# Two normalised matrix layers on eight cores: one PSUM bank set, evictions on the scalar engine, a two-pass output stage, and output writes issued by GpSimd

## The chip, the cores and the metric

The kernel runs on one Trainium2 chip, the same program on all 8 cores, each on its own 2048 of the 16384 rows. The metric is the device time in microseconds of the slowest core. Engine names: PE is TensorE, DVE is VectorE, ACT is ScalarE, POOL is GpSimd, SP is SyncE. A letter q behind a name is the engine's own DMA queue or sequencer.

## The reference, cut to what matters

```
def ln(x): m = mean(x); v = var(x); return (x - m) / sqrt(v + 1e-5)      # over the last axis, 4096
x  = data                                   # [2, 8192, 4096] f32
w1 = weight1 * elem_mask                    # [4096, 4096]; mask in blocks of 32 x 32, a block counts if its sum is > 0
x  = x + ln( ln(x) @ w1.T )
x  = x + ln( ln(x) @ sign(weight2).T + bias )
return x                                    # [2, 8192, 4096] f32
```

## The kernel before

**Tiling.** A core has 2048 rows of x, worked in NCH = 4 chunks of TC = 512 rows, each of NT = 4 tiles of 128 rows (`tt` in the code, tiles 0 to 3 here). Each chunk goes through two layers (`layer` 0 and 1). A layer's weights are 16 slabs (`sl`) of 2 MB in bf16: slab `sl` holds one half (`kh = sl % 2`) of the contraction of 512 output columns (`nsl = sl // 2`). The two slabs of one `nsl` are called a group here, so a layer has groups 0 to 7. For each slab PE runs 4 tiles x 16 matmuls of 128x128 by 128x512 (line 462). A group's product stands in PSUM after the slab with `kh == 1`, one bank of 512 f32 columns per tile.

**PSUM.** All eight banks are used: `pmm` (four banks), `ptA` and `ptB` (two each). Even groups go to pmm. In all layers but the first of chunk 0 (`split`), odd groups go to ptA and ptB (`acc_bank`). ptA and ptB also take the transposes of the normalised rows, 16 per half tile (line 204), so the first transposes of a chunk wait for the last group's eviction (`prev_ev[0]["pt"]`).

**Weights.** Chunk 0 loads f32 weights in pieces of 512 KB through two staging buffers WST. In layer 0 DVE multiplies them with the expanded mask (line 375), in layer 1 ACT takes their sign (line 389); both write a slab buffer WSL (two of them) and POOL stores it to DRAM as c1m or c2m (line 400). Chunks 1 to 3 load these cached slabs, one DMA of 2 MB on SP's queue (line 415) into the buffer that was freed at the end of the slab before last.

**Front of a chunk.** x is loaded in halves of a tile into two buffers XS by POOL (line 517); DVE makes its statistics (lines 548 to 562, `emit_p0_part1`), ACT normalises into HS (lines 582, 586), PE transposes, ACT copies the transposes to HT (line 214). From chunk 1 on tile 0 of this is prepared during the layer before, and PE alternates transposes and the first slab's matmuls tile by tile.

**Eviction.** After a group's second slab DVE copies each tile's bank to ARAW, a bf16 buffer of 4 x 4096 columns (line 483 in layer 0, line 485 with the bias in layer 1), and then makes four statistics over them (line 492). Each evicted tile raises `vEv`; PE waits for it before it uses that bank again. Each finished tile of a group raises `vMM`.

**Between the layers** (`emit_a2`): DVE rescales ARAW, adds x (loaded again by POOL into XS, line 630) into XP, ACT makes sums of squares and the second normalisation.

**Output stage** (`emit_finalize`). At the end of a chunk the result is XP + normalised ARAW. A chain of small operations on DVE (`chain3`), then per tile three passes over 4096 columns on DVE: ARAW in place times a scalar (line 737), OS from XP minus a scalar (line 739), OS plus ARAW (line 742); then ACT issues the write of OS, 2 MB (line 748). OS is one buffer, so each tile waits for the previous tile's write (`sO`). The third pass raises `vFi`.

**Order.** The output stage of chunk c is emitted in layer 0 of chunk c + 1, after slab 0. On DVE it therefore stands behind the statistics of the new chunk's tiles 1 to 3 and ahead of the first eviction (group 0). That eviction waits for `vFi` of all four tiles, since it overwrites ARAW. The last chunk's output stage stands at the very end, by itself.

The rule by which a bank is chosen and guarded is:

```
prev_use = nsl - (2 if split else 1)
if prev_use >= 0:
    wt(t, ev_at.get((prev_use, tt)))
elif nsl == 0 and prev_ev[0] is not None:
    wt(t, prev_ev[0]["pm"][tt])
```

Of the kernel before, what the change touches and what calls it, by code (L numbers as in the profile page):

```python
# [5 lines left out]
try:  # L6
# [11 lines left out]
AF = mybir.ActivationFunctionType  # L18

D = 4096  # L20
TPC = 2048
NCH = 4
TC = TPC // NCH
NT = TC // 128
# [10 lines left out]
        "vDs", "vPs", "vMk", "vTp", "vBi", "vFi", "vXf"]  # L35


def build():
# [16 lines left out]
    with es:  # L55
# [373 lines left out]
        def emit_slab_mm(c, layer, sl, ready, su, ev_at, ht_mark, site,  # L429
                         pre_tt=None, tr_base=0, bank_guard=None):  # L430
            nsl, kh = sl // 2, sl % 2
            mm_marks = {}
            split = not (c == 0 and layer == 0)
# [4 lines left out]
            def _(t):  # L438
# [5 lines left out]
                for tt in range(NT):  # L444
                    if interleave:
                        pre_tt(t, tt)
                        if tt == 0:
                            wt(t, ready)
                    if kh == 0:
                        wt(t, ht_mark(tt))  # L450
                        if split and nsl % 2 == 1 and tt == 0:
                            wt(t, ht_mark(NT - 1))
                        prev_use = nsl - (2 if split else 1)
                        if prev_use >= 0:
                            wt(t, ev_at.get((prev_use, tt)))
                        elif nsl == 0 and prev_ev[0] is not None:
                            wt(t, prev_ev[0]["pm"][tt])
                    for j in range(KTS):
                        st_ap = HT[:, (kh * KTS + j) * 512 + tt * 128:
                                   (kh * KTS + j) * 512 + tt * 128 + 128]  # L460
                        mv_ap = WSL[su % 2][:, j * 512:(j + 1) * 512]
                        ins = t.matmul(acc_bank(split, nsl, tt),  # L462
                                       st_ap, mv_ap,
                                       start=(kh == 0 and j == 0),
                                       stop=(kh == 1 and j == KTS - 1))
                    if kh == 1 and tt < NT - 1:
                        mm_marks[tt] = inc(ins, "vMM", 1)
# [6 lines left out]
            if kh == 1:  # L474
                @blk.vector
                def _(v):
                    wt(v, ("vFi", state["og"]))
                    ins = None
                    for tt in range(NT):
                        wt(v, mm_marks[tt])  # L480
                        dst = ARAW[:, tt * D + nsl * 512: tt * D + (nsl + 1) * 512]
                        if layer == 0:
                            ins = v.tensor_copy(dst, acc_bank(split, nsl, tt))
                        else:
                            ins = v.tensor_tensor(dst, acc_bank(split, nsl, tt),  # L485
                                                  BIASF[:, nsl * 512:(nsl + 1) * 512],
                                                  op=OP.add)
                        ev_at[(nsl, tt)] = inc(ins, "vEv", 1)
                    wt(v, ev_at[(nsl, NT - 1)])
                    for tt in range(NT):  # L490
                        sslot = site * 4 + tt
                        ins = v.bn_stats(BNST[:, sslot * 48 + nsl * 6:  # L492
                                             sslot * 48 + (nsl + 1) * 6],
                                         ARAW[:, tt * D + nsl * 512:
                                              tt * D + (nsl + 1) * 512])
                    if nsl == 7:
                        ev_at["stats_done"] = inc(ins, "vDs", 1)
# [98 lines left out]
        def emit_a2(c, t0, ev_at):  # L596
# [25 lines left out]
            for tt in range(NT):  # L622
# [83 lines left out]
        def emit_finalize(c, ev_at):  # L706
            t0 = c * TC
# [14 lines left out]
            chain3 = ("vSt", cnt["vSt"])  # L722

            fin = {}
            for tt in range(NT):
                my_og = state["og"]
                state["og"] += 1

                @blk.vector
                def _(v, tt=tt, my_og=my_og):  # L730
                    wt(v, chain3)
                    if my_og > 0:
                        v.wait_ge(sem["sO"], 16 * my_og)
                    r3 = RS[:, 12 + tt:12 + tt + 1]
                    mrs3 = AUX[:, 12 + tt:12 + tt + 1]
                    srcr = ARAW[:, tt * D:(tt + 1) * D]
                    ins = v.tensor_scalar(srcr, srcr, r3, None, OP.mult)
                    vds_edge(v, ins)
                    ins = v.tensor_scalar(OS[:, :], XP[:, tt * D:(tt + 1) * D],
                                          mrs3, None, OP.subtract)  # L740
                    vds_edge(v, ins)
                    ins = v.tensor_tensor(OS[:, :], OS[:, :], srcr, op=OP.add)  # L742
                    fin[tt] = inc(ins, "vFi", 1)

                @blk.scalar
                def _(s, tt=tt):
                    wt(s, fin[tt])
                    s.dma_start(out_d[t0 + tt * 128: t0 + (tt + 1) * 128, :],
                                OS[:, :]).then_inc(sem["sO"], 16)
                    cnt["sO"] += 16  # L750

        fin_pending = [None]

        for c in range(NCH):
# [11 lines left out]
            for layer in range(2):  # L766
# [7 lines left out]
                def pre_tt(t, tt, _nm=norm_marks, _sp=single_pt, _c=c,  # L774
# [17 lines left out]
                for sl in range(NSL):  # L792
                    if sl + 1 < NSL:
                        nxt = emit_w_load_prep(c, layer, sl + 1)
                    ready, su = pend
                    emit_slab_mm(c, layer, sl, ready, su, ev_at, ht_mark, site,
                                 pre_tt=pre_tt if sl == 0 else None)
                    if sl == 0:
                        if layer == 0 and fin_pending[0] is not None:
                            emit_finalize(*fin_pending[0])  # L800
                            fin_pending[0] = None
# [7 lines left out]
                if single_pt:  # L809
                    prev_ev[0] = {"pm": {tt: ev_at[(7, tt)] for tt in range(NT)},  # L810
                                  "pt": None}
                else:
                    prev_ev[0] = {"pm": {tt: ev_at[(6, tt)] for tt in range(NT)},
                                  "pt": ev_at[(7, NT - 1)]}
# [50 lines left out]
```

## Time and profile before

| what | us |
|---|---|
| median of the 2 runs | 3339.06 (3338.13 to 3340.0) |
| the profiled execution | 3343.32 |
| its span, slowest core | 3341.9 |
| spans of the other cores | 3298.2 to 3338.4 |
| busy: PE, DVE, ACT, POOL | 2018.1, 890.5, 519.5, 339.9 |

The span runs from the first to the last instruction of a core; the execution's time lies 1.4 us above it. The page gives each engine's busy time over the whole span, but this kernel has stages of very different kinds: chunk 0 (to about 1510 us), where weights are prepared and PE waits for them, then three chunks of which each has a front, a steady layer 0, a stage between the layers and a steady layer 1, and a tail of 68 us. So times are to be read per stage. The mean granted TensorE clock is 0.818 to 0.824 of full speed on all cores.

### The profile page before, as it was taken

The page shows a single profiled execution, that of the slowest core. Times are in us where ns is not written, and L with a number is a line of the kernel's source. Part 1 is how long each engine was busy: PE and PEld are TensorE (multiplying, and loading weights), DVE is VectorE, ACT ScalarE, POOL GpSimd, SP SyncE. Part 2 cuts the span into 40 slices and gives each one's busy share as a digit, 9 for nine tenths or more (in the row PEclk, how much of TensorE's full clock was granted, in tenths as well). Part 3 has the DMA queues.
Part 4 walks back from the last instruction along what each step waited for, and adds up shares of the span by engine and source line. Part 5 has one row for each costly group of instructions (what it writes and reads, how often), then busy time and mean ns, then how long its engine had stood idle before and what let it go on. Part 6 is the DMA issues. An engine that isn't in the chain of part 4 may idle for free.

```text
span 3341.9 us, 24099 instructions; the slowest of 8 cores (3298.2 to 3341.9 us)
## 1 busy us (share of the span) xinstructions
PE 2018.1 (60%) x9272; PEld 930.2 (28%) x9272; DVE 890.5 (27%) x1412; ACT 519.5 (16%) x340; POOL 339.9 (10%) x328
## 2 busy tenths in 40 slices
PE   1033123322633555556895699689669968966991
PEld 0011011110211222223342344334234433423440
DVE  0132122211441100105313221531322144132114
ACT  0120000000025333333002400300240030024000
POOL 4404432343000000000000000000000000000000
PEclk9996567755866777778998899799879989977996
DMA  3456566555743777775544244454424445442442
GB/s 126 129 192 203 192 233 203 165 197 194 237 149 119 222 232 244 220 239 164 203 152 149 105 154 180 166 202 151 151 101 151 176 167 211 151 151 76 151 151 101
DMA packets 72944, 573.12 MB, mean 171 GB/s; under 512 B 8800, under 2 KB 8816, under 8 KB 42112
## 3 DMA queue, kind: packets, MB, share of 16 engines
q1 hardware_dynamic: 51840, 343.96, 31.4%
q0 software_dynamic: 18688, 194.08, 16.7%
q10 hardware_dynamic: 2304, 33.56, 2.5%
q8 instruction: 75, 1.23, 0.2%
q14 instruction: 37, 0.30, 0.0%
HBM read 470.86 MB, written 100.70 MB: 171 GB/s over the span
## 4 chain that ended last, share of the span: by engine, by line
PE 37%; DMA 28%; DVE 12%; ACT 10%; POOL 8%; issue 5%; DVEq 0%; POOLq 0%; ACTq 0%; SPq 0%
PE pmm L462 17%; DMA WST<-w2s 11%; PE ptA L462 9%; PE ptB L462 9%; DMA WST<-w1s 8%; POOL MHI L250 7%; DMA OS<-mask 3%; DMA out<-OS 3%; DVE WSL L375 2%; DVE OS L742 2%; ACT WSL L389 2%; DMA XS<-x 2%; ACT HS L693 2%; ACT HS L662 2%; DVE BNST L548 1%
## 5 line engine op out<-in xcount | busy, mean ns | idle before, releaser
L462 PE MATMUL pmm<-WSL,HT 128*128 128x512 bf16 x4608 | 1103.1, 404 | 279.7 <-ACT WSL L389 105.6
L462 PEld LDWEIGHTS pmm<-WSL,HT 128*128 128x128 bf16 x4608 | 470.8, 103 | 900.0 <-issue 424.8
L462 PE MATMUL ptA<-WSL,HT 128*128 128x512 bf16 x1792 | 409.8, 388 | 105.7 <-ACT WSL L389 104.9
L462 PE MATMUL ptB<-WSL,HT 128*128 128x512 bf16 x1792 | 395.9, 379 | 0.0
L274 PE MATMUL ptB<-COLRED,P4T 128*4 128x512 bf16 x8 | 4.7, 585 | 498.9 <-ACT COLRED L264 498.9
L204 PE MATMUL ptA<-IDN,HS 128*128 128x128 bf16 x576 | 63.8, 299 | 347.8 <-ACT HS L693 237.3
L462 PEld LDWEIGHTS ptA<-WSL,HT 128*128 128x128 bf16 x1792 | 177.8, 100 | 330.0 <-issue 129.0
L462 PEld LDWEIGHTS ptB<-WSL,HT 128*128 128x128 bf16 x1792 | 175.1, 98 | 211.6
L375 DVE TENSOR_TENSOR WSL<-WST,BTE 128x1024 bf16<-128x1024 f32 x128 | 155.5, 1223 | 208.6 <-DMA WST<-w1s 207.6
L389 ACT ACTIVATE WSL<-WST 128x1024 bf16<-128x1024 f32 x128 | 135.0, 1056 | 264.6 <-DMA WST<-w2s 264.4
L485 DVE TENSOR_TENSOR ARAW<-pmm,BIASF 128x512 bf16<-128x512 f32 x64 | 44.0, 691 | 447.9 <-PE pmm L462 447.9
L492 DVE BATCH_NORM_STATS2 BNST<-ARAW 128x6 f32<-128x512 bf16 x256 | 158.3, 681 | 6.6
L204 PEld LDWEIGHTS ptA<-IDN,HS 128*128 128x128 bf16 x576 | 55.6, 138 | 361.8 <-issue 361.8
L662 ACT ACT_TABLE_LOAD x16 | 20.5, 1283 | 864.5 <-DVE XP L655 864.2
L274 PEld LDWEIGHTS ptB<-COLRED,P4T 128*4 128x4 bf16 x8 | 0.6, 80 | 503.3 <-issue 503.3
L250 POOL TENSOR_TENSOR MHI<-MHI 128x1024 int32<-128x1024 int32 (+3 forms) x128 | 125.9, 984 | 18.3
L264 ACT ACT_TABLE_LOAD x8 | 10.3, 1283 | 741.3 <-POOL MHI L250 741.3
L485 DVE TENSOR_TENSOR ARAW<-ptA,BIASF 128x512 bf16<-128x512 f32 x32 | 22.1, 692 | 373.8 <-PE ptA L462 373.8
L288 DVE TENSOR_SCALAR BRT<-ptB 4x512 bf16<-4x512 f32 x8 | 5.4, 679 | 434.6 <-PE ptB L274 434.6
L548 DVE BATCH_NORM_STATS2 BNST<-XS 128x6 f32<-128x512 f32 x128 | 78.4, 679 | 142.1 <-DMA XS<-x 142.1
L630 POOL DMA_DIRECT2D XS<-x x32 | 19.3, 602 | 947.9 <-DVE XP L655 883.2
L214 ACT ACTIVATE HT<-ptA 128x2048 bf16<-128x2048 bf16 x36 | 67.6, 1877 | 277.5 <-PE ptA L204 277.5
(64 smaller groups left out, 1034.9 us busy)
## 6 DMA issues: line engine op xcount, KB each, us to landing
WSL<-c1m SPq DMA_DIRECT2D x48, 2048.0 KB, 9.3
WSL<-c2m SPq DMA_DIRECT2D x48, 2048.0 KB, 7.8
WST<-w1s SPq DMA_DIRECT2D x128, 512.0 KB, 4.7
WST<-w2s SPq DMA_DIRECT2D x128, 512.0 KB, 4.6
XS<-x POOLq DMA_DIRECT2D x56, 1024.0 KB, 6.0
OS<-mask POOLq DMA_DIRECT2D x16, 2048.0 KB, 10.1
XP<-mask POOLq DMA_DIRECT2D x16, 2048.0 KB, 12.7
c1m<-WSL POOLq DMA_DIRECT2D x16, 2048.0 KB, 10.4
```

The costliest lines, as they stand in the source:

```text
L204: ins = t.transpose(pt[:, j * 128:(j + 1) * 128], HS[:, ktg * 128:(ktg + 1) * 128], IDN[:, :])
L214: ins = eng.activation(dst, src, AF.Identity)
L250: ins = g.tensor_tensor(MHI[:, dst_off:dst_off + dst_n], a[:, :, 0], a[:, :, 1], op=OP.add)
L375: ins = v.tensor_tensor(dst, src, mk, op=OP.mult)
L389: ins = s.activation(buf[:, j0 * 512:(j0 + KTQ) * 512], WST[(wfirst + q) % 2][:, :], AF.Sign)
L462: ins = t.matmul(acc_bank(split, nsl, tt), st_ap, mv_ap, start=(kh == 0 and j == 0), stop=(kh == 1 and j == KTS - 1))
L485: ins = v.tensor_tensor(dst, acc_bank(split, nsl, tt), BIASF[:, nsl * 512:(nsl + 1) * 512], op=OP.add)
L492: ins = v.bn_stats(BNST[:, sslot * 48 + nsl * 6: sslot * 48 + (nsl + 1) * 6], ARAW[:, tt * D + nsl * 512: tt * D + (nsl + 1) * 512])
L548: ins = v.bn_stats(bn[:, (hf * 4 + q) * 6: (hf * 4 + q + 1) * 6], xb[:, q * 512:(q + 1) * 512])
L662: ins = s.activation(HS[:, :], XP[:, tt * D:(tt + 1) * D], AF.Square, accum_out=XSQ[:, tt:tt + 1])
L693: ins = s.activation(HS[:, :], XP[:, tt * D:(tt + 1) * D], AF.Identity, bias=AUX[:, 8 + tt:8 + tt + 1], scale=RS[:, 8 + tt:8 + tt + 1])
L742: ins = v.tensor_tensor(OS[:, :], OS[:, :], srcr, op=OP.add)
```

## The change

- `acc_bank` always returns a bank of pmm; ptA and ptB hold transposes only. PE waits for the eviction of the group before (`prev_use = nsl - 1`), tile by tile, and the transposes' extra wait is gone.
- In layer 0 of chunks 1 to 3 ACT evicts (`activation`, Identity) and DVE makes only the statistics. In layer 1, and in chunk 0, DVE evicts as before.
- The eviction of a tile waits for `vFi` of the same tile of the output stage (`fin_war`), no longer for all four. `vFi` is now raised by the first pass; a new semaphore `vFo` is raised by the second, and the stage between the layers and the write wait for that.
- The output stage has two passes per tile: OS = ARAW times a scalar, and OS = (XP minus a scalar) plus OS in one `scalar_tensor_tensor`. ARAW is no longer written by it.
- The write of OS is issued by POOL, no longer by ACT.
- The output stage is emitted in two parts, the small chain before slab 0 and the four tiles before slab 1.

```diff
-        def acc_bank(split, nsl, tt):
-            if split and nsl % 2 == 1:
-                return (ptA if tt < 2 else ptB)[:, (tt % 2) * 512:
-                                                (tt % 2 + 1) * 512]
+        def acc_bank(use8, nsl, tt):
             return pmm[:, tt * 512:(tt + 1) * 512]
...
-                        if split and nsl % 2 == 1 and tt == 0:
-                            wt(t, ht_mark(NT - 1))
-                        prev_use = nsl - (2 if split else 1)
+                        prev_use = nsl - 1
                         if prev_use >= 0:
                             wt(t, ev_at.get((prev_use, tt)))
                         elif nsl == 0 and prev_ev[0] is not None:
-                            wt(t, prev_ev[0]["pm"][tt])
+                            wt(t, prev_ev[0][tt])
...
             if kh == 1:
-                @blk.vector
-                def _(v):
-                    wt(v, ("vFi", state["og"]))
-                    ins = None
-                    for tt in range(NT):
-                        wt(v, mm_marks[tt])
...
+                og4 = state.get("og_pend", -NT)
+
+                def fin_war(eng, tt):
+                    if og4 + tt + 1 > 0:
+                        eng.wait_ge(sem["vFi"], og4 + tt + 1)
+
+                if layer == 0 and c >= 1:
+                    @blk.scalar
+                    def _(s):
+                        for tt in range(NT):
+                            fin_war(s, tt)
+                            wt(s, mm_marks[tt])
+                            dst = ARAW[:, tt * D + nsl * 512:
+                                       tt * D + (nsl + 1) * 512]
+                            ins = s.activation(dst, acc_bank(use8, nsl, tt),
+                                               AF.Identity)
+                            ev_at[(nsl, tt)] = inc(ins, "vEv", 1)
+
+                    @blk.vector
+                    def _(v):
+                        wt(v, ev_at[(nsl, NT - 1)])
+                        ins = None
+                        for tt in range(NT):
+                            sslot = site * 4 + tt
+                            ins = v.bn_stats(BNST[:, sslot * 48 + nsl * 6:
...
+                        vds_edge(v, ins)
...
+                else:
+                    @blk.vector
+                    def _(v):
+                        ins = None
+                        for tt in range(NT):
+                            fin_war(v, tt)
+                            wt(v, mm_marks[tt])
...
-                    wt(v, ("vFi", state["og"]))
+                    wt(v, ("vFo", state["og"]))
...
+        def emit_finalize_tile(c, chain3, tt):
...
+            @blk.vector
+            def _(v, tt=tt, my_og=my_og):
+                wt(v, chain3)
+                if my_og > 0:
+                    v.wait_ge(sem["sO"], 16 * my_og)
...
+                ins = v.tensor_scalar(OS[:, :], srcr, r3, None, OP.mult)
+                araw_free = inc(ins, "vFi", 1)
+                wt(v, araw_free)
+                ins = v.scalar_tensor_tensor(OS[:, :], XP[:, tt * D:(tt + 1) * D],
+                                             mrs3, OS[:, :],
+                                             OP.subtract, OP.add)
+                fin[tt] = inc(ins, "vFo", 1)
+
+            @blk.gpsimd
+            def _(g, tt=tt):
+                wt(g, fin[tt])
+                g.dma_start(out_d[t0 + tt * 128: t0 + (tt + 1) * 128, :],
+                            OS[:, :]).then_inc(sem["sO"], 16)
...
-                    ins = v.tensor_scalar(srcr, srcr, r3, None, OP.mult)
-                    vds_edge(v, ins)
-                    ins = v.tensor_scalar(OS[:, :], XP[:, tt * D:(tt + 1) * D],
-                                          mrs3, None, OP.subtract)
-                    vds_edge(v, ins)
-                    ins = v.tensor_tensor(OS[:, :], OS[:, :], srcr, op=OP.add)
-                    fin[tt] = inc(ins, "vFi", 1)
-
-                @blk.scalar
-                def _(s, tt=tt):
-                    wt(s, fin[tt])
-                    s.dma_start(out_d[t0 + tt * 128: t0 + (tt + 1) * 128, :],
-                                OS[:, :]).then_inc(sem["sO"], 16)
...
-                    if tt == 0 and prev_ev[0] is not None:
-                        pt_m = prev_ev[0].get("pt")
-                        if pt_m is not None:
-                            extra.append(pt_m)
...
+                    if layer == 0 and fin_pending[0] is not None:
+                        fc, fev = fin_pending[0]
+                        if sl == 0:
+                            fin_chain[0] = emit_finalize_chain(fc, fev)
+                        elif sl == 1:
+                            for ftt in range(NT):
+                                emit_finalize_tile(fc, fin_chain[0], ftt)
+                            fin_pending[0] = None
```

How this moves instructions is seen at three places of the front of chunk 1. First PE, from the end of group 0 (slab 1) to slab 2, before:

```order
L462 MATMUL pmm<-WSL,HT 128x512 [waits sWs1]
L462 MATMUL pmm<-WSL,HT 128x512 x63
L437 UNCONDITIONAL_BRANCH
L462 MATMUL ptA<-WSL,HT 128x512 [waits sWs0,vTe]
L462 MATMUL ptA<-WSL,HT 128x512 x15
L462 MATMUL ptA<-WSL,HT 128x512 [waits vTe]
L462 MATMUL ptA<-WSL,HT 128x512 x15
```

The same place after:

```order
L456 MATMUL pmm<-WSL,HT 128x512 [waits sWs1]
L456 MATMUL pmm<-WSL,HT 128x512 x63
L433 UNCONDITIONAL_BRANCH
L456 MATMUL pmm<-WSL,HT 128x512 [waits sWs0,vTe,vEv]
L456 MATMUL pmm<-WSL,HT 128x512 x15
L456 MATMUL pmm<-WSL,HT 128x512 [waits vTe,vEv]
L456 MATMUL pmm<-WSL,HT 128x512 x15
```

Slab 2's matmuls go to pmm and wait for evictions (`vEv`) before each tile's 16; before they waited for none.

Second, DVE around the last tile of the output stage and the first eviction, before:

```order
L737 TENSOR_SCALAR ARAW<-ARAW,RS 128x4096 [waits vSt,sO]
L739 TENSOR_SCALAR OS<-XP,AUX 128x4096 [waits vDs]
L742 TENSOR_TENSOR OS<-OS,ARAW 128x4096 [waits vDs]
L475 UNCONDITIONAL_BRANCH
L483 CAST ARAW<-pmm 128x512 [waits vFi,vMM]
L483 CAST ARAW<-pmm 128x512 [waits vMM] x3
L492 BN_STATS BNST<-ARAW 128x6 [waits vEv]
```

DVE at the same place after:

```order
L765 TENSOR_SCALAR OS<-ARAW,RS 128x4096 [waits vSt,sO]
L768 SCALAR_TENSOR_TENSOR OS<-XP,AUX,OS 128x4096 [waits vFi]
L487 UNCONDITIONAL_BRANCH
L493 BN_STATS BNST<-ARAW 128x6 [waits vEv]
L493 BN_STATS BNST<-ARAW 128x6 x3
```

The evictions have left DVE's queue. On ACT they stand where the four writes stood, behind the last copies of transposes; ACT after:

```order
L609 ACTIVATE HS<-XS,AUX,RS 128x2048 [waits vSt,vTr]
L613 ACTIVATE HS<-XS,AUX,RS 128x2048
L214 ACTIVATE HT<-ptA 128x16x128 [waits vTr]
L214 ACTIVATE HT<-ptB 128x16x128 [waits vTr]
L476 UNCONDITIONAL_BRANCH
L483 ACTIVATE ARAW<-pmm 128x512 [waits vFi,vMM] x4
```

So ACT evicts each tile when both its matmuls and its first pass of the output stage are done.

Third, POOL after the loads of x for the new chunk's tiles 1 to 3 (x6); before, the loads of x for the stage between the layers follow at once:

```order
L517 DMA XS<-x 128x2048 [waits vXf] x6
L623 UNCONDITIONAL_BRANCH
L630 DMA XS<-x 128x2048 [waits vXf] x2
L623 UNCONDITIONAL_BRANCH
L630 DMA XS<-x 128x2048 [waits vXf] x2
```

And POOL after, the last two of the four writes of the output stage, which stand between them:

```order
L776 DMA out<-OS 128x4096 [waits vFo]
L773 UNCONDITIONAL_BRANCH
L776 DMA out<-OS 128x4096 [waits vFo]
L650 UNCONDITIONAL_BRANCH
L657 DMA XS<-x 128x2048 [waits vXf] x2
```

The loads for the stage between the layers now stand behind the four writes.

## Rows read from the trace of the kernel before

**Rows 1.** Head of the page.

```profile
span 3341.9 us, 24099 instructions; the slowest of 8 cores (3298.2 to 3341.9 us)
```

**Rows 2.** Busy time by stage: front, layer 0 of chunk 1, tail; columns in the first row.

```profile
core 3: us, PE busy (x) PEld busy (x) DVE busy (x) ACT busy (x) POOL busy (x), PEclk, DMA share, GB/s
...
1510.00:1625.00 115.00, 74.58 (x384) 37.62 (x384) 58.92 (x88) 26.82 (x14) 3.70 (x6) 0.83 0.59 201
1625.00:1794.00 169.00, 168.74 (x768) 75.76 (x768) 37.51 (x59) 0.00 (x0) 0.00 (x0) 0.98 0.40 150
...
3274.00:3342.00 68.00, 0.18 (x1) 0.00 (x0) 38.47 (x33) 0.00 (x0) 0.00 (x0) 0.52 0.29 123
```

**Rows 3.** Timeline of PE: start, us, instructions, [idle before, ended by].

```profile
1510.86 1.05 PE L204 MATMUL ptA<-IDN,HS 128*128 128x128 bf16 x16 [1.05 <-DVE ARAW L485]
...
1625.27 30.73 PE L462 MATMUL pmm<-WSL,HT 128*128 128x512 bf16 x128 [11.34 <-DVE ARAW L483]
...
1683.46 27.79 PE L462 MATMUL pmm<-WSL,HT 128*128 128x512 bf16 x128
```

**Rows 4.** Chain of waits, chunk 1's front: start, us, what.

```profile
1586.95 14.04 DMA out<-OS
...
1609.44 6.45 DMA out<-OS
```

**Rows 5.** Timeline of DVE, last tile of the output stage, first eviction.

```profile
1615.98 1.29 DVE L737 TENSOR_SCALAR ARAW<-ARAW,RS 128x4096 bf16<-128x4096 bf16 x1 [6.62 <-DMA out<-OS]
1617.38 2.35 DVE L739 TENSOR_SCALAR OS<-XP,AUX 128x4096 f32<-128x4096 bf16 x1
1619.83 4.42 DVE L742 TENSOR_TENSOR OS<-OS,ARAW 128x4096 f32<-128x4096 f32 x1
1624.43 2.48 DVE L483 CAST ARAW<-pmm 128x512 bf16<-128x512 f32 x4 [0.17 <-DVE OS L742]
```

**Rows 6.** Timeline of DVE, fronts of chunks 2 and 3, waits for a write.

```profile
2183.00 1.28 DVE L737 TENSOR_SCALAR ARAW<-ARAW,RS 128x4096 bf16<-128x4096 bf16 x1 [8.80 <-DMA out<-OS]
...
2203.69 1.29 DVE L737 TENSOR_SCALAR ARAW<-ARAW,RS 128x4096 bf16<-128x4096 bf16 x1 [12.41 <-DMA out<-OS]
...
2791.61 1.29 DVE L737 TENSOR_SCALAR ARAW<-ARAW,RS 128x4096 bf16<-128x4096 bf16 x1 [13.32 <-DMA out<-OS]
```

**Rows 7.** Busy time and granted clock just after PE's idle stretch, columns as rows 2.

```profile
1625.20:1628.70 3.50, 3.44 (x9) 1.24 (x10) 3.40 (x6) 0.00 (x0) 0.00 (x0) 0.50 1.01 426
```

**Rows 8.** Timeline of DVE in the tail, first passes of tiles 0 and 1.

```profile
3282.51 1.28 DVE L737 TENSOR_SCALAR ARAW<-ARAW,RS 128x4096 bf16<-128x4096 bf16 x1 [0.18 <-DVE AUX L182]
...
3297.29 1.28 DVE L737 TENSOR_SCALAR ARAW<-ARAW,RS 128x4096 bf16<-128x4096 bf16 x1 [6.50 <-DMA out<-OS]
```

**Rows 9.** Chain of waits: a load issued by POOL, a write by ACT.

```profile
1525.04 0.50 issue
...
3290.84 0.03 issue
3290.87 6.33 DMA out<-OS
```

**Rows 10.** DMAs issued by POOL: XP from mask, then times to landing for mask, XS.

```profile
XP<-mask POOLq DMA_DIRECT2D x16, 2048.0 KB, 12.7
...
DMA to landing us min/median/max: 8.1/10.1/21.9
...
DMA to landing us min/median/max: 4.9/6.1/21.2
```

**Rows 11.** The page's groups: an ACT pass over 1024 elements.

```profile
L389 ACT ACTIVATE WSL<-WST 128x1024 bf16<-128x1024 f32 x128 | 135.0, 1056 | 264.6 <-DMA WST<-w2s 264.4
```

**Rows 12.** DMA issues at 1565 to 1575 us: slab 2's load.

```profile
WSL<-c1m SPq DMA_DIRECT2D x1, 2048.0 KB, 14.2
```

**Rows 13.** Timelines: PE in layer 1 of chunk 0, DVE's statistics of a tile.

```profile
1314.11 15.49 PE L462 MATMUL pmm<-WSL,HT 128*128 128x512 bf16 x64 [12.60 <-ACT WSL L389]
...
1513.11 4.83 DVE L548 BATCH_NORM_STATS2 BNST<-XS 128x6 f32<-128x512 f32 x8
```

More of the change, by code:

```diff
@@ L421, in emit_w_load_prep @@
             return ready, su
-        def acc_bank(split, nsl, tt):
-            if split and nsl % 2 == 1:
-                return (ptA if tt < 2 else ptB)[:, (tt % 2) * 512:
-                                                (tt % 2 + 1) * 512]
+        def acc_bank(use8, nsl, tt):
             return pmm[:, tt * 512:(tt + 1) * 512]
         def emit_slab_mm(c, layer, sl, ready, su, ev_at, ht_mark, site,
-                         pre_tt=None, tr_base=0, bank_guard=None):
+                         pre_tt=None, use8=False, tr_base=0, bank_guard=None):
             nsl, kh = sl // 2, sl % 2
             mm_marks = {}
-            split = not (c == 0 and layer == 0)
             interleave = pre_tt is not None and c >= 1
@@ L474, in emit_slab_mm @@
             if kh == 1:
-                @blk.vector
-                def _(v):
-                    wt(v, ("vFi", state["og"]))
-                    ins = None
-                    for tt in range(NT):
-                        wt(v, mm_marks[tt])
[L481 to L497, printed above, removed]
@@ new lines, in emit_slab_mm @@
+                og4 = state.get("og_pend", -NT)
[20 more added lines that the diff above has]
+                            ins = v.bn_stats(BNST[:, sslot * 48 + nsl * 6:
+                                                 sslot * 48 + (nsl + 1) * 6],
+                                             ARAW[:, tt * D + nsl * 512:
+                                                  tt * D + (nsl + 1) * 512])
+                        vds_edge(v, ins)
+                        if nsl == 7:
+                            ev_at["stats_done"] = ("vDs", cnt["vDs"])
+                else:
[5 more added lines that the diff above has]
+                            wt(v, mm_marks[tt])
+                            dst = ARAW[:, tt * D + nsl * 512:
+                                       tt * D + (nsl + 1) * 512]
+                            if layer == 0:
+                                ins = v.tensor_copy(dst, acc_bank(use8, nsl, tt))
+                            else:
+                                ins = v.tensor_tensor(dst, acc_bank(use8, nsl, tt),
+                                                      BIASF[:, nsl * 512:(nsl + 1) * 512],
+                                                      op=OP.add)
+                            ev_at[(nsl, tt)] = inc(ins, "vEv", 1)
+                        wt(v, ev_at[(nsl, NT - 1)])
+                        for tt in range(NT):
+                            sslot = site * 4 + tt
+                            ins = v.bn_stats(BNST[:, sslot * 48 + nsl * 6:
+                                                 sslot * 48 + (nsl + 1) * 6],
+                                             ARAW[:, tt * D + nsl * 512:
+                                                  tt * D + (nsl + 1) * 512])
+                        if nsl == 7:
+                            ev_at["stats_done"] = inc(ins, "vDs", 1)
@@ L704, in emit_a2, with emit_finalize_chain @@
             return a2_norm
[L706 to L707 removed]
+        def emit_finalize_chain(c, ev_at):
+            state["og_pend"] = state["og"]
             @blk.vector
@@ L797, in build @@
                                  pre_tt=pre_tt if sl == 0 else None)
[L798 to L801, printed above, removed]
                     if c == 0 and layer == 0 and sl % 2 == 0 and sl // 2 + 2 <= 7:
@@ L807, in build @@
                         pend = nxt
[L809 to L814, printed above, removed]
+                prev_ev[0] = {tt: ev_at[(7, tt)] for tt in range(NT)}
                 if layer == 0:
```

28 lines of the change are left out of this document (14 added, 14 removed).

## The prediction

> **What bounds the kernel now.** I read four views, in this order: the head of the page, the busy time by stage, the chain of waits around one suspicious stage, and then the timeline of PE (TensorE) and of DVE (VectorE) in that stage. The span is 3341.9 us on the slowest core [rows 1]. The profiled execution took 3343.3 us with what lies around the span, and the median of the runs shown is 3339.06 us, 4.3 us less.
>
> The stages say where the change can matter [rows 2]. In the long stretches in which the sixteen slabs of a layer run from the cached weights, PE is busy all the time (168.74 of 169 us). There DVE works 37.5 us and ACT (ScalarE) not at all, so whoever evicts there is hidden. In the front of chunk 1 (1510 to 1625 us) PE is busy only 74.58 of 115 us, and in the tail (3274 to 3342 us) it does nothing. The fronts of chunks 2 and 3 look alike. So the change must be judged at three fronts and one tail.
>
> In a front PE first works through group 0 (slabs 0 and 1, in bank set pmm), then group 1 (slabs 2 and 3, in ptA and ptB), and then it stops. Group 2 starts at 1625.27, after 11.34 us of idleness ended by DVE's first eviction [rows 3]. That eviction stands on DVE behind the whole output stage of the previous chunk: four tiles, each of three passes, with only one buffer OS. So each tile waits for the previous tile's write: the chain goes through writes of 14.04 and 6.45 us [rows 4]. DVE's last tile begins at 1615.98, its passes last 1.29, 2.35 and 4.42 us, and the eviction begins at 1624.43 [rows 5]. What bounds a front is this ladder of passes and writes, and the two bank sets let PE do two groups, 128 matmuls beyond group 0, beside it.
>
> **Part 1: one bank set instead of two.** Group 1 now goes to pmm too, so slab 2 needs, tile by tile, the evictions of group 0. In the steady stretches this costs nothing. Tile 0 of a group is finished three tiles before its slab ends; three tiles are 48 matmuls, some 10.4 us at 27.79 us for 128 [rows 3], and one eviction lasts 0.62 us (2.48 for four, [rows 5]). The cover is these 10.4 us; it is gone only if the evicting engine is late by more. In layer 1 DVE takes in tile 0 of the next chunk between two groups, eight statistics (4.83 us, [rows 13]) and a short chain, and that falls into a slab which gives it no eviction. In chunk 0, layer 1, PE waits for weights before each slab anyway, as 12.60 us before slab 9 [rows 13]. I take nothing for both.
>
> In the fronts it costs. Tile 3 of slab 2 cannot start before tile 3 of ARAW has been read by the last tile of the output stage. Behind that moment PE still has tile 3 of slab 2 and all of slab 3, 16 + 64 = 80 matmuls, before it comes to group 2. These had been done beside the ladder. At 27.79/128 = 0.217 us each they are 17.3 us: **+17.3 us per front**. The price of the cold clock stays: after the idle stretch the granted clock is 0.50 of full speed, that is the 1.2 GHz level [rows 7], and the first group takes 30.73 instead of 27.79. This 2.9 us is paid once either way, since a second, earlier stall lies before the wait for the last tile and its slow matmuls are hidden in it.
>
> **Part 2: the eviction's guard and its engine.** The eviction waited for all three passes of all four tiles; now each tile waits for the first pass of its own. From the start of the last tile that is 2.35 + 0.10 = 2.45 us instead of 1624.43 − 1615.98 = 8.45: **−6.0 us per front**. That ACT now evicts is neutral: its 1024-element pass takes 1.056 us [rows 11], so half of it lies between 0.53 and 1.06, against DVE's 0.62 to 0.69. I take 0.65. ACT has nothing queued behind these evictions until the end of the layer. The guard is per tile only because ACT is not behind DVE's passes in order; DVE's statistics still are, and nobody waits for them there.
>
> **Part 3: two passes instead of three.** The removed in-place pass costs 1.40 us a tile with its gap (1617.38 − 1615.98). The new first pass, bf16 to f32 with one scalar, is the form of the old second one, 2.35 us. The new second pass (subtract and add in one, bf16 and f32 in, f32 out) stands in no row. From below it is a pass of 2.35, from above the two old passes together, 6.8; nearest is the old addition with the same two inputs, 4.42 [rows 5], and I take that. Three tiles are on the path of a front, four on the tail's: **−4.2 us per front, −5.6 in the tail**.
>
> The Trainium skill's "Vector Engine (DVE) Microarchitecture Reference" (section "Points that are easy to get wrong") says that this instruction halves its throughput when both SBUF sources are not bf16. Here XP is bf16, so by the rule nothing is halved, which no row of this trace can confirm.
>
> **Part 4: the write is issued by POOL (GpSimd) instead of ACT.** Two things change per write. An ACT write starts 0.03 us after its release; a load on POOL starts 0.50 us after [rows 9]. And the landing: ACT's write of 2 MB lands in 6.33 us when nothing else runs [rows 9]. POOL's loads of 2 MB took at least 8.1 us and those of 1 MB at least 4.9 [rows 10]. So the landing grows by something between 0 and 1.8 us; half of 6.33 for the second megabyte on top of 4.9 gives 8.0 as a ceiling, and I take 7.4, +1.1. Together +1.6 us per write, with ends 0 and 2.3. On the path are three writes in each front, four in the tail: **+4.8 us per front, +6.4 in the tail**.
>
> The Trainium skill ("DMA: Bandwidth & Descriptors", section "Anatomy of one DMA — SWDGE (gpsimd) path") fits such a transfer as 2.0 us plus bytes over 436 GB/s. By estimate that is 6.8 us for 2 MB, so the write would grow by 1.0 us and not 1.6, and the whole sum would be 8 us less. The row of 4.9 us for 1 MB stands 0.5 above the same fit (4.4), so the trace leans to the dearer value.
>
> POOL's queue also holds the x loads for the second half of the layer (two of 1 MB); they stood ahead and now stand behind the four writes. They are needed some 170 us later. Nothing is lost there.
>
> **Part 5: who shares the DMA engines.** In chunks 2 and 3 DVE waited 12.41 and 13.32 us for the third write [rows 6], because slab 4's weights (issued at the end of slab 2) came at the same time; in chunk 1 it waited 6.62 us [rows 5]. Now PE is held inside slab 2, so slab 4's load is issued only after the ladder. The third write runs alone: **−5.8 us in chunk 2, −6.7 in chunk 3**. In its place slab 4's load meets the fourth write and the x loads. A contended weight load took 14.2 us [rows 12]; between the end of slab 2 and that of slab 3 lie 13.8 us and a little cold clock, so this costs 0 to 3 us per front; I take 0.
>
> **Part 6: the transposes' guard.** They waited 1.05 us for DVE's last eviction [rows 3], three times. The front's ladder starts on DVE's own statistics, behind that same eviction, which do not move. Zero.
>
> **The sum.** Chunk 1: 17.3 − 6.0 − 4.2 + 4.8 = +11.9. Chunk 2: 11.9 − 5.8 = +6.1. Chunk 3: 11.9 − 6.7 = +5.2. Tail: the tile's period was 14.78 us (3297.29 − 3282.51, [rows 8]), now −1.4 + 1.6 each, four times: +0.8. In all **+24.0 us**: 3343.3 becomes 3367.3 by the profiled execution, and 3339.06 becomes **3363** by the median. That is 0.7% slower.
>
> **The rivals.**
> A, not slower: the new second pass runs at 2.35 us, not 4.42. Its place is each of the 13 tiles on the path (3 × 3 + 4), its price −2.07 each, −27 us: 3336. It decides from 24.0/13 = 1.8 us saved, a pass below 2.6 us. For it: the one-tensor pass does run that fast. Against: the addition with the same two tensors does not.
> B, clearly slower, within 2%: writes by POOL go on meeting weights. The third writes stay contended (+12.5), each write costs the upper end (+0.7 × 13 = +9), or slab 4 comes late (up to 3 × 3): half to all of 31 us, 3378 to 3394, middle 3386. For it: chunk 1's second write took 14.04 us, the second write of chunk 2 cost DVE 8.80 [rows 6].
> C, slower by over 2%: POOL's writes land as the mask loads into XP do by their median, 12.7 us [rows 10], 5.3 above what I took, in 13 places: +69, 3432; or the second pass takes twice 4.42 us: +57, 3421. For it: only contended rows.
> D, the change does not bring its stall: the evictions come early enough. That needs the fourth tile's first pass 17 us earlier; no row offers it, and I count it in A.
>
> **Chances.** Forecast 0.62, A (with D) 0.12, B 0.21, C 0.05. The range of 8 in 10 is 3338 to 3388: below, the cheapest write (−14) and part of A; above, most of B. A measurement of this kernel tells about 2% (67 us) from no change: faster by over 2% 0.02, within 2% 0.92, slower by over 2% 0.06.
>
> **What would show it.** In the fronts after: ACT's evictions of group 0 spread out with the tiles; PE in slab 2 stalls before tile 2 and again before tile 3, 5 to 11 us each; no stall before group 2; DVE's ladder of 2.35 and 4.42 us passes; the third write in chunks 2 and 3 alone, near 7.5 us; PE without a gap in the steady stretches; the tail's period near 15 us. If PE stalls in steady stretches, part 1 is wrong; if the tail's period falls below 14 us, part 3 or 4 is.

## The result and the profile after

The changed kernel takes 3369.63 us (median), the kernel before 3339.42 beside it on the same chips: ratio 1.0076, interval 1.005 to 1.0103, which is 25 us more (17 to 34). Every kernel here has some executions in which one half of the cores shows a lower clock and takes some per cent longer: the ratios leave these out, the medians do not, and run 6, whose profile is one of them, is read on cores 0 to 3. The forecast was 3363, slower by 0.7%. The mechanism came out as forecast; some terms of the sum had the wrong size, and they cancelled in part.

First the front of chunk 1 on PE, the changed kernel's slowest core (start, us, instructions, [idle before, ended by]); it answers to [rows 3]:

```profile
span 3366.5 us, 24253 instructions; the slowest of 8 cores (3320.0 to 3366.5 us)
...
1562.75 25.82 PE L456 MATMUL pmm<-WSL,HT 128*128 128x512 bf16 x112 [2.29 <-ACT HT L214]
1592.67 5.30 PE L456 MATMUL pmm<-WSL,HT 128*128 128x512 bf16 x16 [4.10 <-ACT ARAW L483]
1607.07 18.94 PE L456 MATMUL pmm<-WSL,HT 128*128 128x512 bf16 x80 [9.11 <-ACT ARAW L483]
1629.12 71.17 PE L456 MATMUL pmm<-WSL,HT 128*128 128x512 bf16 x329 [3.11 <-DMA WSL<-c1m]
```

PE runs 112 matmuls: tile 3 of slab 0, slab 1 and tiles 0 and 1 of slab 2. Then it stands before tile 2 and again before tile 3, each time until ACT's eviction. After the last one come the 80 matmuls of the forecast. The fourth row was not forecast: group 2 waits 3.11 us for slab 4's weights.

The ladder on DVE and the evictions on ACT, same core and front; they answer to [rows 5]:

```profile
1589.43 2.35 DVE L765 TENSOR_SCALAR OS<-ARAW,RS 128x4096 f32<-128x4096 bf16 x1 [10.12 <-DMA out<-OS]
1591.88 4.49 DVE L768 SCALAR_TENSOR_TENSOR OS<-XP,AUX,OS 128x4096 f32<-128x4096 bf16 x1
1603.83 2.35 DVE L765 TENSOR_SCALAR OS<-ARAW,RS 128x4096 f32<-128x4096 bf16 x1 [7.46 <-DMA out<-OS]
...
1574.86 0.60 ACT L483 ACTIVATE ARAW<-pmm 128x512 bf16<-128x512 f32 x1 [1.58 <-PE pmm L456]
1591.93 0.60 ACT L483 ACTIVATE ARAW<-pmm 128x512 bf16<-128x512 f32 x1 [16.47 <-DVE OS L765]
1606.33 0.60 ACT L483 ACTIVATE ARAW<-pmm 128x512 bf16<-128x512 f32 x1 [13.81 <-DVE OS L765]
```

Tile 3's eviction starts at 1606.33, 2.50 us after its first pass began (before: 8.45). The passes last 2.35 and 4.49 us.

The steady stretch and the tail, busy time by stage with columns as in [rows 2]:

```profile
core 5: us, PE busy (x) PEld busy (x) DVE busy (x) ACT busy (x) POOL busy (x), PEclk, DMA share, GB/s
1506.00:1629.00 123.00, 78.29 (x384) 38.56 (x380) 58.12 (x91) 34.16 (x24) 5.31 (x10) 0.82 0.54 185
1629.00:1795.00 166.00, 165.88 (x768) 75.08 (x768) 12.65 (x21) 21.43 (x29) 0.00 (x0) 1.00 0.44 155
3298.00:3366.50 68.50, 0.00 (x0) 0.00 (x0) 33.19 (x29) 0.00 (x0) 2.13 (x4) 0.51 0.29 123
```

PE has no gap in 166 us with one bank set, so the single set costs nothing there.

The whole time of one core also holds chunk 0, whose length differs from core to core by up to 54 us in one execution (45 before, 38 after). So I cut layer 0 of chunks 1 to 3 into three parts from the timelines of PE and DVE, on all 8 cores, and took means: A, from the end of the last matmul of the layer before to the first pass of tile 0 of the output stage; B, the ladder, from there to the first pass of tile 3; C, from there to the end of layer 0's matmuls. The tail runs from the last matmul to the end of the span.

| run | A (chunks 1, 2, 3) | B | C | tail |
|---|---|---|---|---|
| before | 51.1, 50.4, 51.0 | 53.2, 54.1, 53.4 | 177.7, 177.4, 177.4 | 68.0 |
| after | 50.8, 50.9, 51.1 | 47.9, 50.3, 47.4 | 191.5, 190.4, 191.8 | 69.4 |
| one bank set alone | 50.4, 50.2, 50.6 | 50.2, 54.2, 50.4 | 204.9, 204.7, 205.3 | 68.0 |
| two bank sets | 50.7, 50.8, 50.8 | 50.9, 54.2, 51.1 | 169.1, 165.9, 169.1 | 69.3 |
| writes by ACT | 51.0, 50.9, 51.4 | 44.3, 43.0, 42.2 | 188.7, 188.4, 188.8 | 62.3 |
| x loads first | 50.4, 50.8, 51.1 | 46.9, 50.0, 46.6 | 189.2, 188.8, 189.0 | 69.2 |
| two bank sets, writes by ACT | 50.3, 50.7, 51.3 | 48.5, 48.7, 44.8 | 170.1, 169.6, 174.2 | 62.8 |
| old guard (cores 0 to 3) | 50.8, 50.4, 51.3 | 47.9, 47.9, 46.0 | 205.1, 204.7, 204.7 | 69.0 |
| third pass | 50.7, 50.6, 50.9 | 56.3, 56.4, 56.2 | 188.9, 188.8, 188.5 | 79.1 |
| OS in halves | 50.6, 50.6, 51.3 | 38.7, 38.0, 36.8 | 179.6, 180.6, 181.0 | 43.1 |

After minus before: A nothing, B −15.1, C +41.2, tail +1.4, in all some +28 us, inside the +17 to +34 of the ratio. Layer 1 of chunks 1 to 3 has the same length before and after within 1 us.

### The profile page after: what moved, and what is told of

Its sections match the earlier page's. It is cut to its first block, busy times and chain, and to the rows that moved or that the text cites. A ratio compares the mean times of both kernels' runs of the same rounds, so it can differ in the third digit from the quotient of the medians.

```text
span 3366.5 us, 24253 instructions; the slowest of 8 cores (3320.0 to 3366.5 us)
## 1 busy us (share of the span) xinstructions
PE 2028.3 (60%) x9272; PEld 933.6 (28%) x9272; DVE 806.7 (24%) x1300; ACT 607.5 (18%) x460; POOL 347.7 (10%) x344
## 4 chain that ended last, share of the span: by engine, by line
PE 37%; DMA 29%; DVE 11%; ACT 10%; POOL 7%; issue 5%; DVEq 0%; POOLq 0%; ACTq 0%; SPq 0%
PE pmm L456 35%; DMA WST<-w2s 10%; DMA WST<-w1s 8%; POOL MHI L250 7%; DMA OS<-mask 4%; DMA out<-OS 3%; DVE WSL L375 2%; ACT WSL L389 2%; DMA XS<-x 2%; ACT HS L720 2%; ACT HS L689 2%; DVE OS L768 2%; DMA WSL<-c1m 1%; DVE BNST L575 1%; DVE OS L765 1%
## 5 line engine op out<-in xcount | busy, mean ns | idle before, releaser
L456 PE MATMUL pmm<-WSL,HT 128*128 128x512 bf16 x8192 | 1898.8, 397 | 394.4 <-ACT WSL L389 206.5
L456 PEld LDWEIGHTS pmm<-WSL,HT 128*128 128x128 bf16 x8192 | 825.6, 101 | 1458.1 <-issue 575.7
L512 DVE TENSOR_TENSOR ARAW<-pmm,BIASF 128x512 bf16<-128x512 f32 x128 | 88.3, 692 | 906.7 <-PE pmm L456 906.7
L483 ACT ACTIVATE ARAW<-pmm 128x512 bf16<-128x512 f32 x96 | 57.3, 597 | 254.5 <-PE pmm L456 154.7
L657 POOL DMA_DIRECT2D XS<-x x32 | 18.5, 579 | 749.6 <-DVE XP L682 554.6
L544 POOL DMA_DIRECT2D XS<-x x24 | 12.7, 529 | 614.4 <-ACT HS L609 564.9
L768 DVE SCALAR_TENSOR_TENSOR OS<-XP,AUX,OS 128x4096 f32<-128x4096 bf16 x16 | 71.8, 4485 | 1.7
L250 POOL TENSOR_TENSOR MHI<-OS 128x2048 int32<-128x2048 int32 x16 | 57.6, 3599 | 110.5 <-DMA OS<-mask 110.4
## 6 DMA issues: line engine op xcount, KB each, us to landing
OS<-mask POOLq DMA_DIRECT2D x16, 2048.0 KB, 10.4
```

What stands on the lines that cost most here:

```text
L250: ins = g.tensor_tensor(MHI[:, dst_off:dst_off + dst_n], a[:, :, 0], a[:, :, 1], op=OP.add)
L456: ins = t.matmul(acc_bank(use8, nsl, tt), st_ap, mv_ap, start=(kh == 0 and j == 0), stop=(kh == 1 and j == KTS - 1))
L483: ins = s.activation(dst, acc_bank(use8, nsl, tt), AF.Identity)
L512: ins = v.tensor_tensor(dst, acc_bank(use8, nsl, tt), BIASF[:, nsl * 512:(nsl + 1) * 512], op=OP.add)
L768: ins = v.scalar_tensor_tensor(OS[:, :], XP[:, tt * D:(tt + 1) * D], mrs3, OS[:, :], OP.subtract, OP.add)
```

## The experiments

Each ran beside the kernel before on its chip; a ratio is to that. Two runs on different chips are compared by their ratios or by the stages of the table.

**1. Two bank sets again.**

```diff
-            return pmm[:, tt * 512:(tt + 1) * 512]
+            if split and nsl % 2 == 1:
+                return (ptA if tt < 2 else ptB)[:, (tt % 2) * 512:(tt % 2 + 1) * 512]
+            return pmm[:, tt * 512:(tt + 1) * 512]
-                        prev_use = nsl - 1
+                        prev_use = nsl - (2 if split else 1)
```

> The changed kernel with one part undone: odd groups go to ptA and ptB again, with the guards of before; ACT eviction, per-tile guard, two passes and POOL's writes stay. Theory (the single bank set costs the fronts): PE runs groups 0 and 1 beside the ladder of the output stage, and group 2 finds its banks evicted, since tile 3's first pass now comes about 8 us earlier than the first eviction did before. The stalls of before (11.3, 10.5, 11.4 us) and the slow matmuls behind them (2.9 us each) go, 42 us below before, and the tail adds about 1.5: 3299. Rival 1 (the loss is POOL's writes): the fronts stay long, 3350 or more. Rival 2 (ACT's evictions with their table loads cost the loss): 3350 or more too.

Measured: 3300.85 us, ratio 0.9896 (0.9848 to 0.9944). PE on the slowest core, group 1 and group 2 of chunk 1:

```profile
1593.41 7.07 PE L462 MATMUL ptB<-WSL,HT 128*128 128x512 bf16 x32
1602.50 7.07 PE L462 MATMUL ptA<-WSL,HT 128*128 128x512 bf16 x32 [2.02 <-DMA WSL<-c1m]
1609.40 7.07 PE L462 MATMUL ptB<-WSL,HT 128*128 128x512 bf16 x32
1616.31 27.79 PE L462 MATMUL pmm<-WSL,HT 128*128 128x512 bf16 x128
```

Group 2 follows without a stall; what is left is a late weight load (slab 3's here). Both rivals fall: POOL's writes and ACT's evictions are still in it. Per front the stages give 11 us less than before, where 14 was expected. PE still waits for weights, 0.9 us per front (waits of over 1.5 us); the rest of the 3 us was not followed up. The rest of the change is worth −1.0% by itself, and the single bank set turned that into +0.8%.

**2. The single bank set alone, on the kernel before.**

```diff
-            split = not (c == 0 and layer == 0)
+            split = False
...
-                if single_pt:
+                if True:
```

The second line drops the transposes' extra wait, which no longer has a bank to guard.

> The kernel before with one part of the change: all groups go to pmm (no odd groups in ptA and ptB), all else as before. Theory: slab 2 now waits for DVE's first eviction, behind all four tiles of the output stage, and the 128 matmuls of group 1 come after it: 27.6 us per front, 83 in all; the third write of chunks 2 and 3 runs without a weight load beside it (-12.5), the weight load of slab 4 comes late by some 2 us per front (+7): 3339 + 78 = 3417. Rival (the bank set is worth little, the time went elsewhere): below 3360.

Measured: 3416.29 us, ratio 1.0242 (1.0208 to 1.0275). PE, front of chunk 1 on the slowest core:

```profile
1575.24 20.09 PE L462 MATMUL pmm<-WSL,HT 128*128 128x512 bf16 x80 [2.29 <-ACT HT L214]
1625.82 74.39 PE L462 MATMUL pmm<-WSL,HT 128*128 128x512 bf16 x338 [30.50 <-DVE ARAW L483]
```

PE stands 30.50 us after group 0 instead of 11.34 after group 1. C grows by 27.5 us, the 128 matmuls (27.6). The two smaller terms came out otherwise and nearly cancel: B falls by 5.9 us in all and not by 12.5, and PE nowhere waits over 1.5 us for slab 4's weights, for which 7 had been set. So what a bank set buys is the number of matmuls that it lets run beside the ladder.

**3. The writes issued by ACT**, placed between the evictions of group 0.

```diff
-            @blk.gpsimd
-            def _(g, tt=tt):
-                wt(g, fin[tt])
-                g.dma_start(out_d[...], OS[:, :]).then_inc(sem["sO"], 16)
+            # in ACT's block of group 0: write 0, evictions 0 and 1, write 1,
+            # eviction 2, write 2, eviction 3, write 3
+                wt(s, fin[tt])
+                s.dma_start(out_d[...], OS[:, :]).then_inc(sem["sO"], 16)
```

> The changed kernel with the writes of the output stage issued by ACT again, each placed between the evictions of group 0 so that none waits for another's write (write 0, evictions 0 and 1, write 1, eviction 2, write 2, eviction 3, write 3). Theory: POOL costs 0.5 us to start and 0.25 us to land per write, 0.75 x 9 = 6.8 in the fronts, 3 in the tail, and the 3.7 us between the last landing and the end of the span: 3370 - 13 = 3356. Rival 1 (POOL's writes are the whole loss): 3339. Rival 2 (the price is nothing): 3369.

Measured: 3340.89 us, ratio 1.001 (0.9981 to 1.0038). That is less than the changed kernel by 22 us by the ratios and by 30 by the stages, not by 13. The tail gained 7.1, as expected. The fronts gained 23, where I had expected 7. The chain of waits in the tail, first POOL's write in the changed kernel:

```profile
3327.03 0.53 issue
3327.56 6.56 DMA out<-OS
...
3350.82 4.50 DVE OS L768
3355.36 0.48 issue
```

and ACT's, on core 1 of this run:

```profile
3287.34 6.31 DMA out<-OS
3293.74 2.36 DVE OS L771
3296.20 4.50 DVE OS L774
3300.77 6.30 DMA out<-OS
```

In the tail a write by POOL costs 0.5 us to start and 0.25 to land: DVE waits 7.31 instead of 6.50 (means over the cores). In the fronts DVE's three waits add up to 27.0, 29.4 and 26.6 us after, 23.5, 22.2 and 21.4 here. Of those 16 us less 7.3 (9 x 0.81) are the write's own price by the tail. In a front the price can be higher: the third write has no other transfer of its core beside it, and lands after 7.30 us in the changed kernel, after 6.66 in run 2, where ACT issues it (means of 24). By that some 10 of the 16 are the price. The rest goes with contention: the first two writes of a front share 4.9 and 7.8 us with a weight load in the changed kernel and 3.8 and 4.4 here. And C fell by 2.6 per front. The edit does a second thing: the x loads no longer stand behind writes on POOL, and PE waits for weights over 1.5 us only once in 24 fronts (13 times in the changed kernel; run 5 takes this up). In the number, then, the dearer writes could be called the whole loss (that was rival 1); but run 1 shows as well that the bank set could. With ACT's writes the ladder's gain (B −10.4 on the mean) just pays for the bank set (C +11.1).

**4. Both: two bank sets and ACT's writes.**

> The changed kernel with two bank sets and with ACT's writes, both as in the two runs before: what is left of the change is two passes, the per-tile guard and ACT's eviction. Theory: in the fronts the ladder is hidden beside groups 0 and 1, so quicker writes give nothing there and only the tail gains 6.6 us on the two-bank version: 3292, faster than both kernels. Rival: if the fronts of the two-bank version are still bound by the ladder, it gains 6.8 us more there, 3285.

Measured: 3297.85 us, ratio 0.9889 (0.9853 to 0.9925). In the layers 0 the mean length is 269.4 us against 270.9 in run 1, although the ladder is 2 to 6 us shorter. The two times are too near for the intervals to tell 3292 from 3285, so the waits decide: PE waits for an eviction over 1.5 us once in the 24 fronts of run 1 and never here, and 0.9 of the 1.5 us are run 1's waits for weights. With two sets the ladder is hidden, and a quicker write gives little but the tail (62.8 against 69.3).

**5. The x loads ahead of the writes.**

```diff
+            # POOL, before the four writes:
+            g.dma_start(XS[u % 2][:, :], x_d[t0: t0 + 128, hf * 2048:(hf + 1) * 2048])   # hf 0, 1
```

> The changed kernel, with the first two x loads of the stage between the layers put ahead of the four writes on POOL again, as they stood before the change; nothing else. Theory: slab 4's weight load, which now ends late and stalls PE (1.5 us per front over the eight cores of the profiled execution), shares the DMA engines with these two loads; ahead of the writes they run beside slab 2's load, which has time. The stall goes, -4.5 us in all: 3365. Rival (the fourth write alone makes slab 4 late, or the early loads make write 0 longer by as much): 3370 or more, with the stall still there or the wait for write 0 above 10 us.

Measured: 3355.93 us, ratio 1.0049 (1.0012 to 1.0086); the interval overlaps the changed kernel's, so the stages decide: B and C together fell by 9 us. DMA issues of the changed kernel at 1560 to 1640 us (KB each, us to landing):

```profile
out<-OS POOLq DMA_DIRECT2D x4, 2048.0 KB, 8.7
WSL<-c1m SPq DMA_DIRECT2D x4, 2048.0 KB, 12.4
XS<-x POOLq DMA_DIRECT2D x2, 1024.0 KB, 20.7
```

In that front the chain goes through slab 4's load:

```profile
1607.07 5.14 PE pmm L456 x16
1612.33 16.44 DMA WSL<-c1m
```

Issued at the end of slab 2, it meets the fourth write and the two x loads and takes 16.44 us, where slab 3 lasts 13.8. PE's waits of over 1.5 us for weights sum to 36.8 us over the 24 fronts of the changed kernel (8 cores, 3 fronts; 1.5 each) and to 10.0 here. C fell by 2.3, 1.6 and 2.8 us to 189, next to the 188.6 of run 3. So most of the late load is due to the two x loads moved behind the writes, and not to the fourth write alone.

**6. The old guard on the evictions.**

```diff
-                    if og4 + tt + 1 > 0:
-                        eng.wait_ge(sem["vFi"], og4 + tt + 1)
+                    if og4 + NT > 0:
+                        eng.wait_ge(sem["vFo"], og4 + NT)
```

> The changed kernel with the old guard: every eviction of group 0 (still on ACT) waits for the second pass of all four tiles. Theory: the first eviction comes 4.6 us after tile 3's first pass, and tiles 0 to 2 of slab 2 (48 matmuls, 10.4 us), which the per-tile guard let run inside the ladder, come after it: +15 per front; slab 4's load then finds the DMA engines free (-1.5 to -2.5): +38 to 40 in all, 3408. Rival (the guard per tile is worth only the one pass that the last eviction no longer waits for): +4.6 per front, 3383.

Measured: 3412.23 us, ratio 1.0172 (1.0105 to 1.024), by the ratios some 32 us more than the changed kernel; the interval is wide. PE in the front of chunk 1, core 3:

```profile
1562.60 18.84 PE L456 MATMUL pmm<-WSL,HT 128*128 128x512 bf16 x80 [2.29 <-ACT HT L214]
1610.81 69.53 PE L456 MATMUL pmm<-WSL,HT 128*128 128x512 bf16 x308 [29.36 <-ACT ARAW L483]
```

Nothing runs inside the ladder. On cores 0 to 3 C grew by 13.5 us per front (204.8 against 191.3) and B fell by 0.7. So the guard per tile is worth some 13 us per front, of which only 4.6 is the pass that is no longer waited for.

**7. A third pass.**

```diff
-                ins = v.scalar_tensor_tensor(OS[:, :], XP[...], mrs3, OS[:, :], OP.subtract, OP.add)
+                ins = v.tensor_scalar(OS[:, :], OS[:, :], mrs3, None, OP.subtract)
+                vds_edge(v, ins)
+                ins = v.tensor_tensor(OS[:, :], OS[:, :], XP[...], op=OP.add)
```

> The changed kernel with its second pass split in two (OS minus the scalar in place, then OS plus XP), which adds some 2.3 us to each tile of the output stage. Theory: the ladder is on the path with three tiles in each front and four in the tail, 13 in all: +30, 3399, in layer 0 about +7 each and in the tail +9. Rival (the fronts are bound by something else, only the tail by the ladder): +9, 3379.

Measured: 3390.12 us, ratio 1.013 (1.0063 to 1.0198). The new pass, on the page of groups by line:

```profile
L765 DVE TENSOR_SCALAR OS<-ARAW,RS 128x4096 f32<-128x4096 bf16 x16 | 37.7, 2353 | 106.6 <-DMA out<-OS 105.9 <-DVE AUX L182 0.5
L768 DVE TENSOR_SCALAR OS<-OS,AUX 128x4096 f32<-128x4096 f32 x16 | 37.6, 2353 | 1.7
```

Layer 0 grew by 5.7, 4.2 and 5.3 us, the tail by 9.7, in all 25 of the 30 expected. So the ladder is on the path of fronts and tail. B grew by 7.8 us per front, the three passes and a little more; what is given back lies in C, 2.5 us per front: PE no longer waits over 1.5 us for slab 4's weights in any front.

**8. OS in halves**, on version 4.

```diff
+                for hf in range(2):
+                    if my_og > 0:
+                        v.wait_ge(sem["sO1" if hf else "sO"], 16 * my_og)
+                    o = OS[:, hf * 2048:(hf + 1) * 2048]
+                    lo = tt * D + hf * 2048
```

> The version with two bank sets and ACT's writes, with OS used as two halves: each tile is passed and written in halves of 2048 columns, each half with its own semaphore, so that a half is worked while the other is written. Theory: in the fronts the ladder is hidden already, nothing changes; in the tail the period falls from 13.45 (6.95 of DVE and 6.5 of waiting) to DVE's 7.2, and one half's write of some 4 us stays at the end: 62.3 becomes about 41, so 3298 - 21 = 3277, faster than all. Rival (halved writes land no sooner than whole ones, some 6 us each): the tail stays above 50, 3288.

Measured: 3280.47 us, ratio 0.981 (0.9759 to 0.9861). The tail's chain of waits on the slowest core:

```profile
3257.77 1.30 DVE OS L781
3259.16 2.36 DVE OS L787
3261.59 3.89 DMA out<-OS
3265.58 1.30 DVE OS L781
3266.97 2.36 DVE OS L787
```

The tail is 43.1 us instead of 62.8: a tile's period is 7.81, of which DVE works 7.3. The forecast had been 41. The fronts stay as they were (269.1 us per layer 0 against 269.4), although B is 9.5 us shorter: the ladder is hidden there. The version beats both kernels: by its ratio it is 1.9% (1.4 to 2.4%) below the kernel before.

## Why the prediction was right, and where its sum was not

By its own steps, per front from the table (before to after):

- **Part 1, the bank set (+17.3) and part 2, the guard (−6.0)**: together +11.3 in C. Measured +13.7, and +11.1 with the x loads out of the way (run 3). Right, and runs 2 and 6 test the two terms: 27.5 us for 128 matmuls where the same reckoning says 27.6, and some 13 us for the guard together with the 48 matmuls it lets run (0.217 x 80 is 17.4, not 17.3). PE without a gap in the steady stretch was right too. The stall before tile 2 was 4.10 us on the slowest core, just under the 5 to 11 announced.
- **Part 2, the engine**: ACT's eviction lasts 0.60 us (0.65 taken). That it is neutral fits run 1, but no run puts the evictions back on DVE alone.
- **Part 3, the passes**: the unknown pass lasts 4.49 us, beside the 4.42 taken. Right.
- **Part 4, POOL's writes**: mis-sized. The step took +1.6 us per write; the tail shows DVE's wait at 7.31 us against 6.55 before, +0.76; the third write of a front, alone on its core, shows some +1.1 (run 3). The error is in the landing: 6.56 us in the tail, not 7.4. The value had been drawn from loads of 1 MB, which always ran two at a time, and bounded by loads of 2 MB; those took 8.1 us alone, so a load by POOL was no measure of its write. The lower end of the step, 0, left out the start of 0.5 us that it had itself. The Trainium skill's fit ("DMA: Bandwidth & Descriptors", section "Anatomy of one DMA — SWDGE (gpsimd) path") gives 6.8 us for 2 MB by estimate and was nearer. The start, 0.5 us, was right.
- **Tail**: forecast +0.8, measured +1.4, by two errors: four writes cheaper by 0.8 each (the period is 14.25 us where 15 was announced, 14.83 before), and a price that was not in the sum, since after the last landing of a POOL write the span goes on for 4.0 us (the write issued at 3355.87 lands after 6.56 at 3362.4, the span ends at 3366.5; it is 4.0 on every core of each profile here with POOL's writes, and 0.5 before and 0.3 in run 3, where ACT issues them).
- **Part 5, sharing of the DMA engines**: mis-sized twice. The relief of the third write was taken from one core (12.41 and 13.32 us, and none in chunk 1). Over the eight cores that wait was 10.0, 8.4 and 10.8 us before and is 7.6, 7.9 and 8.3. With parts 3 and 4 the ladder was forecast to change by +0.6, −5.2, −6.1 and changed by −5.3, −3.8, −6.0. And slab 4's late load, taken at 0 of "0 to 3", cost 2.6 (2.2 by run 5). Part 4 had said of the x loads that nothing is lost by their new place, since nobody needs them soon; run 5 shows that most of this loss came from them.
- **Part 6, the transposes' guard**: zero, right (A unchanged).

Sum of the fronts: forecast +23.2, measured +26. That it came so near is partly luck: the ladder fell by 15.1 us in all and not by 10.7, and slab 4's load added 7.8 that the sum had at 0. Rival A falls with the 4.49 us pass. Of rival B the late slab 4 came, the dearer writes did not, and the third writes were hardly contended (7.6 to 8.3 us). Rival C did not occur.

Not tried: the two passes alone and ACT's evictions alone on the kernel before, and a single bank set with six or seven banks shared otherwise.

## What to carry to other kernels

A second set of accumulators is not worth what it hides in the steady loop (here nothing) but the matmuls it lets run ahead of one late release: count them behind the stall, at 0.216 us each, and that is its price. When a queue entry is moved past others, look also at what is now issued late and whom it meets: two loads that nobody awaited delayed one that PE did. And a serial ladder of passes and writes can be broken by halving its one buffer: in the tail that gave 19.7 us, where a whole pass more per tile (run 7) moved it by 9.7.

## What the runs showed of the hardware

- **Contention by phase.** DVE's wait for the second write was 7.8 us with ACT's writes and 9.8 to 11.4 with POOL's in the changed kernel, though in the tail the two differ by 0.8. The second write shared 4.4 us with a weight load in the one and 7.8 in the other. On single cores of the changed kernel that wait lies between 7.5 and 15.7 us, so a term read on one core of one run is no measure of it.
- **A table load before each group of evictions.** ACT loads its table again in each of the 24 blocks of evictions, though the function is the same; groups by line, changed kernel:

```profile
L483 ACT ACTIVATE ARAW<-pmm 128x512 bf16<-128x512 f32 x96 | 57.3, 597 | 254.5 <-PE pmm L456 154.7
L483 ACT ACT_TABLE_LOAD x24 | 30.8, 1283 | 363.9 <-PE pmm L456 363.9
```

It starts only when the group's first tile is ready, so it delays that eviction by 1.28 us; the 10.4 us of cover hide it here.
- **The cold clock** cost less than before the change. Busy time and granted clock after the second stall, columns as in [rows 2]:

```profile
1607.00:1610.50 3.50, 3.43 (x9) 1.30 (x10) 3.50 (x1) 0.00 (x0) 0.00 (x0) 0.55 0.02 5
1610.50:1614.00 3.50, 3.50 (x18) 1.59 (x17) 2.65 (x5) 0.00 (x0) 1.60 (x3) 1.00 0.56 225
```

The clock was near its 1.2 GHz level for one stretch of 3.5 us only, after a stall of 9.11 us with 5.30 us of work ahead of it; before, after 11.34 us of idleness, the first 3.5 us had 0.50 [rows 7] and the next 3.3 us only 0.61. The 80 matmuls took 18.94 us where 17.3 are the full clock's: 1.6 us and not the 2.9 that part 1 called the same either way.
